# A state-space layer and an FFN in one kernel: the dt pieces, the Exp of the running sums and the end of the norm in other slots

## What is computed

```python
dt = jax.nn.softplus(dt_raw + dt_bias)
dA = dtc * A                                   # per chunk
dA_cum = jnp.cumsum(dA, axis=2)                # the running sums
decay_states = jnp.exp(dA_cum[:, :, -1:, :] - dA_cum)
chunk_decay = jnp.exp(dA_cum[:, :, -1, :])
Y_off = einsum('bzcn,bzhpn,bzch->bzchp', Cc, prev, jnp.exp(dA_cum))
```

## Time and profile before

| | |
|---|---|
| median of 3 runs | 1892.75 us (1892.32 to 1896.9) |
| the profiled execution | 1896.46 us |
| its span | 1894.7 us |
| mean granted TensorE clock | 0.933 |
| busy: PE, DVE, ACT, POOL | 1689.6, 1388.5, 933.2, 991.4 us |

### The profile page before, as it was taken

The page is one execution under the profiler, slowest core; times in us unless marked ns, Lnnn a source line. Parts: engine busy times, 40 slices in busy tenths (PEclk is TensorE's granted clock), DMA queues, the critical chain, the costliest instruction groups (busy, mean ns, idle before and its releaser), DMA issues. The chain is left out here.

```text
span 1894.7 us, 36975 instructions
## 1 busy us (share of the span) xinstructions
PE 1689.6 (89%) x11168; PEld 841.3 (44%) x11168; DVE 1388.5 (73%) x2200; ACT 933.2 (49%) x1647; POOL 991.4 (52%) x1031
## 2 busy tenths in 40 slices
PE   2698899889899889988989988887899999999998
PEld 1244445434444444543544444454344444444443
DVE  6859758858857875985885787685777777777775
ACT  3463364344435236435443523532776666666662
POOL 0036426525625643652562554374676776767774
PEclk9899899898899889989989988988999999999999
DMA  6111141132014014113202401642011111101111
GB/s 214 49 41 34 37 101 37 29 65 72 26 49 107 26 37 100 43 25 76 60 28 54 100 26 42 158 119 36 28 45 57 34 46 57 56 28 51 34 34 56
DMA packets 214679, 109.66 MB, mean 58 GB/s; under 512 B 133796, under 2 KB 185696, under 8 KB 214496
## 3 DMA queue, kind: packets, MB, share of 16 engines
q1 hardware_dynamic: 214496, 107.37, 21.5%
HBM read 80.57 MB, written 26.76 MB: 57 GB/s over the span
## 5 line engine op out<-in xcount | busy, mean ns | idle before, releaser
L772 PE MATMUL ps_in<-u_hi,w_hi 128*128 128x512 f16 (+1 forms) x608 | 246.7, 406 | 79.7 <-DVE u_lo L1259 32.6
L1077 ACT ACTIVATE decay<-ps_d 128x512 f32<-128x512 f32 x256 | 150.4, 592 | 331.3 <-PE ps_d L830 291.1
L794 PE MATMUL ps_in<-w_out,zg 128*128 128x512 f32 x512 | 254.4, 654 | 22.3 <-DVE pre L1272 22.2
L1359 DVE TENSOR_TENSOR mix<-decay,gb 128x512 f32<-128x512 f32 x256 | 223.7, 879 | 60.2 <-ACT gb L1064 23.8
L1665 POOL TENSOR_TENSOR xend<-xpad,decay 128x256 f32<-128x256 f32 x256 | 184.2, 737 | 146.1 <-PE ps_yo L865 113.9
L772 PE MATMUL ps_in<-u_lo,w_hi 128*128 128x512 f16 (+1 forms) x608 | 245.8, 404 | 0.0
L772 PE MATMUL ps_in<-u_hi,w_lo 128*128 128x512 f16 (+1 forms) x608 | 245.3, 404 | 0.0
L1272 DVE SCALAR_TENSOR_TENSOR pre<-ps_in,cws,pre 128x511 f32<-128x511 f32 (+2 forms) x240 | 179.1, 747 | 41.4 <-ACT pre L1016 35.6
L1758 POOL TENSOR_TENSOR gate_sum<-gate_sum,gate_part 128x512 f32<-128x512 f32 x88 | 142.2, 1616 | 103.4 <-DVE gate_part L1586 103.2
L794 PEld LDWEIGHTS ps_in<-w_out,zg 128*128 128x128 f32 x512 | 104.7, 210 | 173.4 <-issue 170.7
L1016 ACT ACTIVATE pre<-ps_in,cb,cws 128x512 f32<-128x512 f32 x80 | 62.2, 778 | 211.9 <-PE ps_in L772 211.8
(11 more groups left out here) (181 smaller groups left out, 3760.0 us busy)
## 6 DMA issues: line engine op xcount, KB each, us to landing
ebc<-e_dram SPq DMA_DIRECT2D x256, 64.0 KB, 2.6
u<-u_t SPq DMA_DIRECT2D x9, 1024.0 KB, 5.1
res<-u_tok SPq DMA_DIRECT2D x32, 256.0 KB, 2.7
x_dram<-res SPq DMA_DIRECT2D x32, 256.0 KB, 2.0
xa<-x_dram SPq DMA_DIRECT2D x8, 1024.0 KB, 5.8
xr<-x_dram SPq DMA_DIRECT2D x32, 256.0 KB, 2.7
out<-xr SPq DMA_DIRECT2D x32, 256.0 KB, 2.0
fw_words<-gu_words SPq DMA_DIRECT2D x32, 176.0 KB, 2.6
```

Of the source, the lines that this page charges most:

```text
L772: last = mm(ps_in[bk][0:m, :], w[:, k, col:col + m], u[:, k, :], start=(k == 0 and j == 0), stop=(k == KT - 1 and j == 2))
L794: last = mm(ps_in[bk][:, :], zg[:, k, tt * P:(tt + 1) * P], w_out[:, k, :], start=(k == 0), stop=(k == CT - 1))
L1077: ac(decay[:, n % NG, :, :].rearrange("p a b -> p (a b)"), ps_d[n % 2][:, :], ACT.Exp).then_inc(e_done, 1)
L1359: v.tensor_tensor(mix[:, n % NG, :, :], decay[:, n % NG, :, :], gb[:, c % 2, 0:CH].unsqueeze(1).broadcast_to([P, CT, CH]), ALU.mult).then_ ...
```

## The change

The scan and the cast of the running sums go from VectorE's slot 21 to 19, `dt_third` from slot 25 to 21, the Exp of the running sums and the logarithm from ScalarE's slot 23 to 20. The end of the norm goes from 5 slots behind the output tile to 9: from slots 17 and 25 to 21 and 29; the third stays in the tail. SP's store of a norm tile and load of a residual tile go with it, from slots 18 and 26 to 22 and 30. The store of the parts goes from slot 26 to 22 and the loads of the head from 29 to 28. No instruction is added or removed, and the prologue stays as it is.

```diff
--- before.py
+++ after.py
@@ -61,9 +61,9 @@
 W_NEEDED = {"dt": 1, "x0": 2, "x4": 3, "z0": 4, "z4": 5}
 DT_STEPS = 25
 DT_PART = [1, 3, 7, 12, 16]
-DT_SLOT = {7: 0, 9: 1, 13: 2, 17: 3, 21: 4}
+DT_SLOT = {7: 0, 9: 1, 13: 2, 17: 3, 19: 4}
 SPLIT_SLOT = {1: (0, 1), 2: (2, 3)}
-NORM_AT, NORM_END = 3, 5
+NORM_AT, NORM_END = 3, 9
 DEC = 352
 NEG = -1.0e30
 LOG1P = [2.0 / (2 * k + 1) for k in range(8)]
@@ -672,9 +672,9 @@
                         load_ebc(b, (0, 2, 9, 17).index(n))
                     if n == 0:
                         load_dec(b)
-                    if n == 26 and st.proj is not None:
+                    if n == 22 and st.proj is not None:
                         store_parts(b + 1)
-                    if n == 29 and st.proj is not None:
+                    if n == 28 and st.proj is not None:
                         load_head(b + 1)
                     for k, part in DECODE_AT[st.kind].get(n, []):
                         if part == 3:
@@ -1091,7 +1091,7 @@
                     use_in(st, n)
                     if st.proj is not None and n == 6:
                         exp_dt(st.proj)
-                    if st.proj is not None and n == 23:
+                    if st.proj is not None and n == 20:
                         exp_cs(st.proj)
                         ln_dt(st.proj)
                 tail(st)
@@ -1477,7 +1477,7 @@
                             dt_first(st)
                         if n in DT_SLOT:
                             dt_second(st.proj, DT_SLOT[n])
-                        if n == 25:
+                        if n == 21:
                             dt_third(st.proj)
                     for k, part in DECODE_AT[st.kind].get(n, []):
                         decode(b, k, part)
```

## The result

The changed kernel took **1847.0 us** (median of 4 runs, 1842.2 to 1848.8) against 1892.5 us for the kernel before (4 runs, 1891.1 to 1896.9): a ratio of 0.9753, 95% interval 0.9738 to 0.9769. I had forecast 1861 with a range from 1848 to 1878. In the traces the span falls by 47.7 us, from 1894.7 to 1847.0.

A forecast was written before the change was run, and what follows sets the result against it. The prediction took TensorE, busy 89%, and its waits, headed by xpad, as the bound. Seven stages at 4.6 us (32.2) plus 0.5 for the last stage, off the 1892.75 us median, gave 1861, range 1848 to 1878.

The forecast's parts named there:

- the xpad list: TensorE's total wait for ScalarE's copy into xpad (L821), forecast to fall from 44.6 to about 19 us.
- the short new waits: TensorE in slots 24 and 25 would wait for VectorE's yoff, res and state, each under 1 us.
- the unchanged 3.35 us of slot 31: Gap behind res in slot 31; its growth from a late VectorE at slot 30 would show the prediction wrong.
- the wait for yoff in slot 20: TensorE's wait at L865, 1.76 us before, was to fall under 0.7 us.
- the term of 4.6 us a stage: Gain up to the next state matmul after slot 25, the middle of 5.1 and 4.1 us; seven stages give 32.2.
- the order on VectorE from the taps of x2 to yoff of chunk 5: Instruction-by-instruction schedule from 336.6 to 351.2, ending when TensorE wants the state matmuls: no gap or some tenths.
- The norm out of slot 17: Moving the norm's end lets yoff and x2's taps in slot 20 finish 1.2 us sooner, bounds 0.8 and 2.2.
- The relief of slot 25: VectorE, without the norm's end and dt piece (2.2 and 3.15 us) in slot 25, keeps up through slots 26 to 28.
- The stores: Earlier stores of the parts and head loads on SP's queue, costed at 0.
- The table load: ScalarE's second load, 1.28 us: cost 0 even if delayed; with drain, two switches take 5.3 us, total gain 3 us smaller.
- Outside slots 20 and 25: The last stage loses one norm end from slot 17, 0 to 2 us, taken as 0.5; the program's second part is untouched.
- The second rival: Clock stays at 2.4 GHz in slot 20 too and all contention falls away: 6.5 us a stage, 1847 us; chance 0.09.

The follow-up runs named there:

- experiment 3: The changed kernel with the norm's end put back (NORM_END 5): 1849.4 us, ratio 0.9771 against the kernel before.
- (1): The kernel before with only Exp and logarithm moved to ScalarE's slot 20 and the scan to VectorE's slot 19: 1895.7 us, ratio 1.0009.
- (5): The changed kernel with the last dt piece back in slot 25, stores in slot 26 and head loads in 29: 1890.9 us, ratio 0.9989 against the kernel before.
- (7): The kernel before with only the last dt piece moved, to the end of slot 26: 1894.0 us, ratio 1.0009.
- experiment 4: The changed kernel with the stores of the parts back in SP's slot 26 and the head's loads in 29: 1846.3 us, ratio 0.9753 against the kernel before.

## Why the prediction was off

- *The place and the mechanism.* Right: slot 25's wait for xpad, 3.76 us with 1.7 us of slow clock behind it, was the gain: 36.1 us, 5.16 a stage, of the total. Of the signs that I had named, the xpad list (20.0 us, forecast 19), the hidden Exp and logarithm, the short new waits and the unchanged 3.35 us of slot 31 came true; the wait for yoff in slot 20 did not fall under 0.7 us (1.07), and a stage took 150.2 us, not 152.3.
- *The step that failed*, in size, is the term of 4.6 us a stage, which measured 5.86. Under it lies the order on VectorE from the taps of x2 to yoff of chunk 5, and what I drew from it, "VectorE is just about as late as TensorE". From the end of x2's taps to the end of yoff I had 14.6 us (336.6 to 351.2). It took 13.3 (332.57 to 345.84). The scan was the largest part: 0.68 us instead of 1.53, and with its casts 2.35 us instead of 3.2, since GpSimd had no work beside it in slot 19. I had taken its length from a row with GpSimd beside it, while I wrote that no GpSimd instruction is fed there. So yoff ended 1.2 us ahead of TensorE's state matmuls at 347.02, res ended at 348.43, 0.6 us before x4 began at 349.07, and only 0.21 us were left at the state.
- *The mean of two outcomes.* I took 4.6 us a stage as the middle between 5.1 with the full clock in slot 25 and 4.1 with a fallen one. The traces show the full clock there, behind gaps of 0.2 us. Measured were 5.86 for slots 20 and 25, 0.70 and 5.16. So of the 1.26 us that a stage gave more than I had, 0.5 come from the averaging and 0.8 from VectorE's order: 1.3 sooner there, 0.5 less from slot 20.
- *The norm out of slot 17* I had at 1.2 us, with 0.8 as the lower bound. Measured by TensorE's wait for yoff it gave 0.69 (1.76 to 1.07), below the bound, and the output tile came 0.7 us sooner as well. Slot 20 is 0.9 to 1.0 us shorter in six stages and 0.9 longer in the first, 0.70 on average; the clock over the slot makes up the difference (0.87 instead of 0.76 to 0.77 in the six, 0.77 instead of 0.88 in the first). The dt piece's first instruction took 2.22 us, exactly the norm's price, where I had 1.6. Rows 5 to 7 had shown this hold; I gave it too little. Left where it was (experiment 3), the norm's end costs 2.4 us in all, which the intervals don't tell from nothing.
- *The relief of slot 25.* I wrote in one sentence that VectorE "keeps up through slots 26 to 28", and gave it no price. It keeps up but for the 0.92 us of slot 28. Experiments 1, 3, 5 and 7 show that this relief is the other half: ScalarE's move without the dt piece's gave 0 us (1), or 1.6 with the norm's move beside it (5); the dt piece's alone 0 (7); both, with the norm's end left in place, 43 (3). The two paths bound the stage side by side. My sum never asked what slot 28 would do if the piece had stayed; that this did no harm to it is owed to the change holding both moves.
- *The stores:* right, nothing (experiment 4). *The table load:* right, hidden, and made before the decay's input was there. The 3 us less that I had worked out beside it didn't come, and didn't follow from my own times: with 5.3 us for the two switches ScalarE would have been through at 345.3, still ahead of the decay's input at 345.5.
- *Outside slots 20 and 25* I had 0.5 us and the traces show 6.7. Of it 6.8 are slot 12 on the full clock in four stages, where nothing of the change is; 2.5 were lost in other slots, and 2.4 won outside the stages: 3.1 from the last stage on, less 0.8 in the prologue. From slot 0 of the last stage to the end the fourteen kernels took 680 to 687 us, with no clear tie to where the norm stands, so I don't call that part of the gain explained. Why slot 12 turned fast in those four stages is open too.
- *The range* ended at 1848, at the case with every gap and the clock won. It had no room for the clock in slots that the change doesn't touch.
- *A slip in the sum:* 1892.75 less 32.7 is 1860, not 1861.

The second rival comes out nearest, by its time of 1847. But of what it names only slot 25 came true; slot 20 kept its slow clock, at 0.81, and GpSimd's hold in slot 17 stayed at 2.22 us. That its figure was met is chance.

## What to carry to other kernels

When an engine's stall is about to be removed, ask which other engine arrives just behind it: here ScalarE's path and VectorE's path ran side by side, VectorE's only 1.3 us ahead of what TensorE needed (before the change its taps of x4 ended at 369.07, and the output tile began at 370.38), and either move alone was worth nothing. Move small pieces of work to where the engine that shares the memory port is idle, and take their durations from rows with the same neighbour; behind a long instruction of that neighbour the first in line pays, whichever it is. A change of a few microseconds in a repeated stage can shift the clock's slow stretches by as much again, in places that it doesn't touch.

## What the runs showed of the hardware

- The same gap of 1.92 us in the same slot (slot 12) had a slow output tile behind it in stages 1 and 2 of the changed kernel and a fast one in stages 3 to 6 (clock 0.79 and 1.00 over 8 us); in the kernel before it was slow in six stages of seven. Four added matmuls, 0.86 us in a stage, made the kernel before faster by 4.3 us.
- These VectorE instructions, with their operands in SBUF, were held until 0.3 us after the end of GpSimd's multiplication of the state: 2.22 us for L1300 (0.42 alone), 2.23 for L1321 (0.41), 2.22 for L1427 (0.54). Two mixes there took 4.08 us (0.69 each alone). The Trainium skill, "SBUF — State Buffer", section SBUF: two separate sides, calls the port pair of the two engines an exclusive lock for the whole instruction; the rows agree. VectorE's instructions that read PSUM kept their time beside GpSimd's work: 0.68 us for yoff and the state additions, 0.75 for a tap.
- The activation table load at 336.24 started 5.5 us before the input of its Exp was there.
